# Attention: the values' products of the last key tile between the two score pairs of a step

## What is computed

```python
        q = apply_axial_rope(q, pos_map)
        k = apply_axial_rope(k, ctx_pos_map)
        scale = 1.0 / np.sqrt(HEAD_DIM).astype(np.float32)
        logits = jnp.einsum('bqhd,bkhd->bhqk', q, k) * scale
...
        attn = jnp.einsum('bhqk,bkhd->bqhd', w, v)
        attn = attn.reshape(b, n, N_HEADS * HEAD_DIM)
        return attn @ Wout + bout
```

## Time and profile before

| what | value |
|---|---|
| median of 3 runs | 1810.77 us (1808.63 to 1811.18) |
| the profiled execution, its own time | 1811.14 us |
| its span in the profile | 1809.3 us |
| mean granted TensorE clock | 0.926 of full speed |
| PE busy | 1491.6 us (82%) |
| DVE busy | 1366.2 us (76%) |
| ACT busy | 911.2 us (50%) |
| POOL busy | 689.3 us (38%) |

### The profile page before, as it was taken

The page is one execution under the profiler, slowest core; times in us unless marked ns, Lnnn a source line. Parts: engine busy times, 40 slices in busy tenths (PEclk is TensorE's granted clock), DMA queues, the critical chain, the costliest instruction groups (busy, mean ns, idle before and its releaser), DMA issues. The chain is left out here.

```text
span 1809.3 us, 20906 instructions
## 1 busy us (share of the span) xinstructions
PE 1491.6 (82%) x6523; PEld 615.7 (34%) x6523; DVE 1366.2 (76%) x2030; ACT 911.2 (50%) x1201; POOL 689.3 (38%) x477
## 2 busy tenths in 40 slices
PE   5998998886654872899889988999899289898997
PEld 1333333332232321433343344324433134343433
DVE  6989999899988853789668756957792788647453
ACT  4766565664430100447655752776375353546453
POOL 3999999999925335000100010001001033333342
PEclk8898999988986996879999999999999699999999
DMA  6455455555568744300000000000000810000000
GB/s 237 127 149 146 142 144 144 149 149 137 147 187 180 157 96 157 123 1 1 1 1 1 1 1 1 1 1 1 1 1 1 178 46 1 24 1 24 1 24 24
DMA packets 65211, 131.54 MB, mean 73 GB/s; under 512 B 11328, under 2 KB 11328, under 8 KB 64336
## 3 DMA queue, kind: packets, MB, share of 16 engines
q1 hardware_dynamic: 53056, 104.07, 20.3%
q0 software_dynamic: 7168, 25.17, 6.1%
q10 hardware_dynamic: 4880, 0.95, 0.3%
HBM read 134.11 MB, written 12.85 MB: 81 GB/s over the span
## 5 line engine op out<-in xcount | busy, mean ns | idle before, releaser
L363 POOL TENSOR_TENSOR ssm_dBu<-ssm_du,ssm_BC 128x1024 f32<-128x1024 f32 x128 | 303.4, 2375 | 17.2 <-DVE ssm_du L399 17.2
L258 PE MATMUL ssm_psY<-ssm_hC,ident 128*128 128x512 f32 x512 | 256.0, 631 | 47.7 <-POOL ssm_hC L370 33.6
L1493 DVE TENSOR_REDUCE att_next_mx<-att_next_ring 128x1 f32<-128x512 f32 x384 | 242.0, 684 | 32.6 <-PE att_next_ring L1236 31.0
L327 ACT ACTIVATE ssm_dA<-ssm_delta,ssm_negA 128x512 f32<-128x512 f32 x256 | 165.4, 682 | 170.0 <-DVE ssm_hC L419 168.6
L1390 ACT ACTIVATE att_next_Pr<-att_next_psT 128x1024 f32<-128x1024 f32 x192 | 186.3, 1023 | 88.5 <-PE att_next_psT L1260 87.9
L1631 POOL TENSOR_TENSOR mlp_both<-mlp_first,mlp_third 128x512 f32<-128x512 f32 x88 | 124.3, 1412 | 256.9 <-DVE mlp_first L1833 166.1
L1833 DVE SCALAR_TENSOR_TENSOR mlp_first<-mlp_psQ,mlp_s_gu,mlp_first 128x512 f32<-128x512 f32 x176 | 131.4, 749 | 110.2 <-ACT mlp_first L1725 94.0
L1507 POOL TENSOR_TENSOR X<-X,att_bout 128x512 f32<-128x512 f32 x12 | 15.9, 1354 | 496.2 <-SPq L1141 496.2
L464 DVE TENSOR_TENSOR_SCAN ssm_dA<-ssm_dA,ssm_dBu 128x512 f32<-128x512 f32 x144 | 174.3, 1220 | 21.8 <-ACT ssm_dA L327 15.3
L1657 PE MATMUL mlp_psQ<-mlp_xh,mlp_Vgu 128*128 128x512 f16 x352 | 141.5, 402 | 50.4 <-ACT mlp_Vgu L1713 27.6
L258 PEld LDWEIGHTS ssm_psY<-ssm_hC,ident 128*128 128x128 f32 x512 | 96.5, 198 | 197.2 <-issue 93.6
(11 more groups left out here) (316 smaller groups left out, 2488.2 us busy)
## 6 DMA issues: line engine op xcount, KB each, us to landing
ssm_BC<-bc_rows SPq DMA_DIRECT2D x128, 512.0 KB, 4.8
moe_W<-in_masksT POOLq DMA_DIRECT2D x32, 512.0 KB, 8.4
mlp_words<-in_gate_upT SPq DMA_DIRECT2D x32, 176.0 KB, 7.3
X<-in_x SPq DMA_DIRECT2D x4, 1024.0 KB, 10.7
rows<-moe_XP SPq DMA_DIRECT2D x4, 1024.0 KB, 14.6
out_x<-X SPq DMA_DIRECT2D x4, 1024.0 KB, 4.2
mlp_Wd<-in_downT SPq DMA_DIRECT2D x8, 352.0 KB, 14.8
ssm_ctxP<-in_ctxT SPq DMA_DIRECT2D x4, 512.0 KB, 12.3
```

The lines of the kernel that those rows point to most:

```text
L258: nc.tensor.matmul(psY[:, w, :], ident[:], hC[:, w, g % RC, :], start=False, stop=(n == DS - 1)).then_inc(summed, 1)
L327: nc.scalar.activation(dA[:, q % RA, :], delta[:, b % 2, e, :], ACT.Exp, scale=negA[:, e, n:n + 1]).then_inc(dA_done, 1)
L363: nc.gpsimd.tensor_tensor(dBu[:, g % RB], du[:, b % 2, hh * W:(hh + 1) * W, :], BC[:, g % RING, 0, :].unsqueeze(1).broadcast_to([P, W, S]) ...
L1493: nc.vector.tensor_reduce(mx[:, m % 3, qt, row_order(j)], bank(("score", i)), AX.X, ALU.max).then_inc(maxed, 1)
```

## The change

In the loop over the steps of `batch`, the block that issues V stands between K0 (with s1 and the pieces of the output projection) and K1, where it stood behind K1 and s2. Nothing else differs: the same instructions, the same waits, the same `ring_order`, and the queues of the other engines are the same row by row.

```diff
                                 if piece_at(g, kt, 1, ob):
                                     project_out(*piece_at(g, kt, 1, ob))
+                                if here and kt >= 1:
+                                    values(g, kt - 1)
+                                elif g >= 1 and kt == 0:
+                                    values(g - 1, NT - 1)
                                 if here:
                                     key_scores(g, kt, 1)
                                 if ahead:
                                     score(g + LAG, kt, 2)
-                                if here and kt >= 1:
-                                    values(g, kt - 1)
-                                elif g >= 1 and kt == 0:
-                                    values(g - 1, NT - 1)
                                 if ahead:
                                     score(g + LAG, kt, 3)
```

## The result

| | before | after |
|---|---|---|
| median | 1810.97 us (1808.63 to 1811.93, 4 runs) | 1862.96 us (1861.09 to 1863.94, 4 runs) |
| span of the profiled execution | 1809.3 us | 1862.1 us |
| ratio after / before | | 1.0288, 95% interval 1.0270 to 1.0306 |

What follows compares the result with a forecast made beforehand. A loop over one reduction and V, 2.56 us, was taken to set the regular step. Four batches, each losing 7.7 with scores and 5.8 without, gave 54, so 1865 us, 3.0% slower; own range 1853 to 1885.

Steps and rivals of the forecast that it cites:

- The loop over one reduction and V: In regular steps with scores, one reduction and V set the step: 2.56 us before, 3.00 with K1 inside it.
- The stretch with scores: First V of a batch to V of group 5, kt=3: 63.92 us grows to 72.10, net +7.7 a batch.
- the credit for the first V: At a batch's start, the first V comes 0.5 us earlier, no longer waiting for K1 and s2.
- The walk through a group: In a group with scores, V to V of 3.61, 3.61, 3.00, 3.00, together 13.22 us.
- Groups 6 and 7: Steps without scores: V waits for K1's exponential, 2.72 us a step; 19.64 becomes 25.44, +5.8 a batch.
- the step with the copy of psO: At kt=1 in groups 6 and 7, the copy lies between K1's exponential and V: 3.20 us, two such steps.
- The forecast of 54: Over all four batches, 4 x (7.7 + 5.8) = 54 us lost.
- (a): Rival: only the groups without scores lose, 4 x 5.8 = 23, giving 1834 us; chance 0.06.
- (b): Rival: only the stretch with scores loses, 4 x 7.7 = 31, giving 1842 us; chance 0.06.
- (c): Rival: no change, 1811 us, as the most loaded engine, VectorE, keeps the time; chance 0.04.
- (d): Rival: faster, 1802 us, V filling the 0.18 wait of s2 in regular steps; chance 0.03.
- (e): Rival: TensorE's clock falls because it idles; products twice as long in groups 6 and 7, 1919 us; chance 0.05.

Runs made afterwards that it cites:

- the two runs of the parts: Against before, V ahead of K1 only in steps with scores: 1845.94 us; only in groups 6 and 7: 1834.56 us.
- the three kernels that share the loop: After, V ahead of K1 in scored steps only, and V between K1 and s2: ratios to before 1.0288, 1.0200 and 1.0211.

## Why the prediction was right

*The bound.* The loop over one reduction and V was read rightly: the step follows it in after (2.99 for 3.00), V behind K1 (2.99), V behind s3 (2.56) and with half reductions (2.73), each forecast before it was seen.

*The stretch with scores.* 72.10 was forecast for it, less 0.5 for an earlier first V: +7.7 a batch. Measured are 71.82, +7.9, and a first V about 0.3 nearer to the last one of the batch before: +7.6. The stretch came out shorter than the walk and the credit for the first V smaller, and the two errors nearly cancel. The walk through a group gave 13.22; it is 13.17 (3.59, 3.59, 3.00, 2.99).

*Groups 6 and 7.* +5.8 was forecast, +6.03 measured. The term that was off is the step with the copy of psO: 3.20 taken, 3.30 measured. The way from ScalarE's end to V was put at 0.06 as for an exponential; behind the copy it is 0.15 (1056.23 + 0.59 to 1056.97).

*The sum.* 4 x 13.93 = 55.7 in the batches. The gaps between them take 1.0 less (84.12, 83.49, 83.17 for 84.44, 83.78, 83.54), which is what the earlier first V makes of it. The time behind the last V takes 1.9 less (1862.1 - 1438.3 = 423.8 for 1809.3 - 1383.6 = 425.7); nothing there is changed, and it took from 420.6 to 426.1 us in the profiled runs. That leaves 52.8, the difference of the spans; the medians lie 52.0 apart. The forecast of 54 was for the batches. That the whole lies a little below it and not above is chance, as the parts outside the V's vary by more. The text of the bounds works out 1890 for the upper one, while the forecast's own range is given as 1853 to 1885; the measured time lies in both.

*The rivals.* (a) and (b), one of the two losses alone, are the two runs of the parts: both losses are there. (c), no change because VectorE is the most occupied engine, fell: its work is 59.24 us (59.51 in the slightly wider window of the earlier trace rows) and its stretch grew from 63.92 to 71.82. The Trainium skill, Perfetto Trace Analysis, "Identifying the Most-Contended Engine", has the engine of the highest occupancy named first. A shorter reduction does help in both kernels (1.0288 falls to 1.0081, 1 to 0.9882), but the loss by V's place stays, though smaller, and occupancy doesn't tell that TensorE's order can slow a stretch in which no engine is full. (d), faster, fell: the wait did not go, it moved from s2 to s1 and grew from 0.18 to about 0.6. (e), the clock falls, did not happen: the granted clock was 1.00 between the V's of the kernel after, with that wait in each regular step.

## What to carry to other kernels

When products alternate with reductions through a ring of three banks, as here, look for a loop: the way from one score through its reduction to the score three places on, and the long product that stands between. Put the long product right behind a score and right ahead of one, so that nothing else is inside the loop. What TensorE can do during the reduction belongs ahead of the waiting score, not behind the long product. And an operation that feeds another engine's queue goes ahead of a long one that only waits for that queue.

## What the runs showed that I had not expected

The stretch of a batch repeats within 0.1 us from batch to batch and from kernel to kernel (71.82 to 71.87 in the three kernels that share the loop), while the gaps between the batches and the stages outside vary by up to 5 us. In the profiled runs with whole reductions a gap goes with the granted clock in it: 82.6 to 84.5 us at 0.98 (all gaps of before and after among them), 84.1 to 85.7 at 0.96, and 85.6 to 87.3 at 0.94, as where V stood behind K1 and the gap was 86.7. So a part of what the experiments lose beyond their batches goes with the clock in the gaps; why the clock was lower there in some kernels is not shown.

With V ahead of K0, TensorE waits longest of all ahead of the V's of kt=1 in groups 6 and 7. In batch 1, behind the one of group 7, with 2.18 us idle ahead of it and 1.60 ahead of each of the two V's before, the key scores lasted 0.64 in place of 0.38, and the interval to the next V was 4.02 in place of 3.64, at a granted clock of 0.64; behind that V they were back:

```profile
1105.73 1.06 PE L1270 MATMUL att_next_psO<-att_next_Pr,att_V 128*32 128x512 f32 x8 [2.18 <-ACT att_next_OT L1364]
1106.73 0.56 PE L1257 MATMUL att_next_psT<-att_QT,att_KT 64*128 64x512 f16 x2
1107.09 0.64 PE L1260 MATMUL att_next_psT<-att_next_nmT,att_pick 64*128 64x512 f16 x2
1107.51 0.64 PE L1257 MATMUL att_next_psT<-att_QT,att_KT 64*128 64x512 f16 x2
...
1109.75 1.27 PE L1270 MATMUL att_next_psO<-att_next_Pr,att_V 128*32 128x512 f32 x8
1110.96 0.39 PE L1257 MATMUL att_next_psT<-att_QT,att_KT 64*128 64x512 f16 x2
```

That is rival (e) in small: two intervals of that batch, longer by 0.4 and 0.2 us. In the other three batches the clock fell at the V of kt=1 in group 6 too: the interval behind it is 4.68 to 4.94 us, at a granted clock of 0.64 to 0.66. In batch 1 it stayed at 1.00 there, though the 1.85 us of idle time ahead of that V are the same in all four, so the wait alone doesn't settle it. The Trainium skill, TensorE: Matmul & The Clock Gate, "Part 1: The HAM clock gate", has the low level as the default that activity lifts. The trace agrees in that the low level (1.2 GHz for 2.4, pairs of products 1.7 times as long) came back where TensorE had waited most. In the kernel after, with about 0.6 us waited in each regular step of 3.00, the granted clock stayed at 1.00.
